# A state-space and expert layer on one core: x turned by a transfer, part of one ScalarE product given to GpSimd, and the small stages laid anew

## The reference, cut to what matters

```python
x = x[:, ::2, :]                               # 32 batches, 750 -> 375 rows, 256 wide; segments of 128
h = softmax(x @ x.T / 16) @ x                  # in each of 3 segments (the last one is padded with zeros)
# selective scan
x_in, z = split(layernorm(h) @ W_in.T)         # 512 and 512 wide
u = silu(conv4(x_in) + b_conv);  dt = softplus(u @ W_dt.T + b_dt)
Bm, Cm = u @ W_B.T, u @ W_C.T                  # 16 states each
for t in rows:                                 # for each state n of 16, each channel of 512
    hid[n] = exp(dt[t] * A[n]) * hid[n] + (dt[t] * u[t]) * Bm[t, n]
    y[t] = sum_n hid[n] * Cm[t, n]
h = h + (y * silu(z)) @ W_out.T
# experts: sigmoid scores of 64 experts, 4 of 8 groups, 8 experts per row, 256 slots each
h = h + experts(layernorm(h))
```

## Time and profile before

| | us |
|---|---|
| median of 3 runs | 3411.68 (3406.43 to 6037.72) |
| the profiled execution | 3408.89, of which 3407.0 from its first to its last instruction |
| up to the first scan | 71 |
| the 32 batches' scans | 71.3 to 2868.8 |
| rest of the sequence phase | until about 2915 |
| count and expert phases | about 2915 to 3407 |

### The profile page before, as it was taken

How to read it: one execution, slowest core, us unless ns; L and a number is a source line. 1 busy time by engine, 2 the same in 40 slices (tenths; PEclk the granted TensorE clock), 3 DMA queues, 4 the chain that set the end, 5 groups by cost and what they waited for, 6 DMA issues and landing times. The chain is left out here.

```text
span 3407.0 us, 56637 instructions
## 1 busy us (share of the span) xinstructions
PE 2969.6 (87%) x19009; PEld 2397.3 (70%) x19009; DVE 2858.1 (84%) x4628; ACT 2823.4 (83%) x5457; POOL 2105.5 (62%) x780
## 2 busy tenths in 40 slices
PE   6899999999999999999999999999999987566664
PEld 4677777777777777777777777777777776455543
DVE  4888999999999999999999999999999997444442
ACT  5999999999999999999999999999999996211110
POOL 0666666666666666666666666666666665177776
PEclk8999999999999999999999999999999998588887
DMA  2111121212112111122222212112221111377774
GB/s 94 52 52 52 55 63 63 63 63 63 58 60 63 56 52 58 63 63 63 63 63 63 64 63 63 59 59 63 63 63 63 59 54 32 94 151 147 149 149 82
DMA packets 187455, 240.52 MB, mean 71 GB/s; under 512 B 45152, under 2 KB 165440, under 8 KB 187200
## 3 DMA queue, kind: packets, MB, share of 16 engines
q1 hardware_dynamic: 162624, 199.44, 18.7%
q0 software_dynamic: 24576, 37.77, 6.6%
HBM read 176.07 MB, written 61.08 MB: 70 GB/s over the span
## 5 line engine op out<-in xcount | busy, mean ns | idle before, releaser
L360 POOL TENSOR_TENSOR hid<-hid,c_all 128x1536 f32<-128x1536 f32 x512 | 1770.4, 3458 | 1100.4 <-DVEq L616 1094.9
L621 DVE TENSOR_TENSOR_SCAN hid<-decay,hid,psB 128x1024 f32<-128x1024 f32 x512 | 1201.4, 2347 | 88.7 <-PE psB L932 42.4
L392 ACT ACTIVATE decay<-dt,a_neg 128x383 f32<-128x383 f32 x2048 | 1086.4, 606 | 0.4
L380 ACT ACTIVATE dbu_t<-dtu_t,b_t 128x512 f32<-128x512 f32 x1536 | 993.2, 714 | 7.5 <-PE psB L932 7.4
L932 PE MATMUL psB<-ident,dbu_t 128*128 128x128 f32 x6144 | 856.5, 276 | 108.4 <-DVE hid L621 102.7
L932 PEld LDWEIGHTS psB<-ident,dbu_t 128*128 128x128 f32 x6144 | 699.0, 141 | 248.5 <-issue 122.7
L944 PE MATMUL psY<-ident,hid 128*128 128x128 f32 x6144 | 757.1, 273 | 1.7 <-POOL hid L360 1.7
L944 PEld LDWEIGHTS psY<-ident,hid 128*128 128x128 f32 x6144 | 689.7, 141 | 2.0 <-POOL hid L360 1.9
L621 DVE TENSOR_TENSOR_SCAN hid<-decay,psB 128x512 f32<-128x512 f32 x512 | 623.3, 1217 | 15.5 <-PE psB L932 10.7
L1019 PE MATMUL psM<-u,w_dt 128*128 128x384 f32 x1024 | 353.2, 488 | 3.4 <-ACT u L424 2.7
L1434 ACT ACTIVATE e_side<-e_psL,e_in_tile 128x128 f32<-128x128 f32 x128 | 45.8, 363 | 260.1 <-DVE e_in_tile L1558 259.4
(11 more groups left out here) (148 smaller groups left out, 3294.3 us busy)
## 6 DMA issues: line engine op xcount, KB each, us to landing
c_all<-bc_rows_dram SPq DMA_DIRECT2D x128, 768.0 KB, 4.8
out_dram<-h SPq DMA_DIRECT2D x64, 384.0 KB, 5.6
h<-out_dram SPq DMA_DIRECT2D x32, 384.0 KB, 3.6
x_weights_dram<-normed SPq DMA_DIRECT2D x32, 384.0 KB, 2.6
xs<-in_x_dram SPq DMA_DIRECT2D x32, 256.0 KB
e_wg<-in_gate_dram SPq DMA_DIRECT2D x64, 128.0 KB, 2.7
e_wu<-in_up_dram SPq DMA_DIRECT2D x64, 128.0 KB, 3.0
e_wd<-in_down_dram SPq DMA_DIRECT2D x64, 128.0 KB, 3.4
```

The costliest lines, as they stand in the source:

```text
L360: nc.gpsimd.tensor_tensor(hid[k % 4][:, :, :], hid[k % 4][:, :, :], c_all[:, k, :].unsqueeze(1).to_broadcast([P, CH, L]), ALU.mult).then_i ...
L380: last = nc.scalar.activation(dbu_t[k % 2][:, t, :], dtu_t[q][:, t, :], ACT.Copy, scale=b_t[q][:, t, k:k + 1])
L392: last = nc.scalar.activation(decay[k % 4][:, c, 1:L], dt[q][:, c, 1:L], ACT.Exp, scale=a_neg[:, c, k:k + 1])
L621: nc.vector.tensor_tensor_scan(h[:, lo:hi], flat(decay[k % 4])[:, lo:hi], flat(psB)[:, lo:hi], h[:, lo - 1:lo] if j else 0.0, ALU.mult, AL ...
```

## The change

It does five things, all in the sequence phase.

1. **x by a transfer.** The host hands over a second, transposed copy of x (`x_t`); SP loads it into a new tile `xt` (two chunks of 128 partitions x 375). `turn_x`, QT0 and QT1 and their two copies go. The factor 1/16 moves into the scale of the softmax exponential, and `row_max` gets a second DVE instruction, on 3 columns, which multiplies by -1/16.
2. **GpSimd part.** In the states 3, 4, 12, 13 and 14 (`POOL_PART`) ACT scales two thirds of `dbu_t`, and POOL the last third, by a `tensor_tensor` with B broadcast along 512 columns. It stands on POOL's queue behind `times_c` of three states earlier. The POOL loop is unrolled.
3. **Carriers.** All `sem_inc(s_turn, 1)` go.
4. **Copies.** XN0 and XN1 are copied by ACT instead of DVE.
5. **Steps and banks.** Most small stages stand at other steps, and names at other places of the two banks.

```diff
+POOL_PART = (3, 4, 12, 13, 14,)
+SLOTTED = (("XN0", "X0", "X2T1", "X2", "Z0", "LG", "Z2", "D0", "D1", "D3", "CB", "BT", "AT1", "YT1", "X2T0",
+            "DU1", "O0"),
+           ("O1", "XN1", "X1", "X3", "Z1", "YT0", "D2", "S", "PT", "AT0", "DU0", "YT2", "DU2"))
...
+                sp.dma_start(xt[:, :, 0:(S + DIL - 1) // DIL],
+                             w["x_t"][a].rearrange("(k p) t -> p k t", p=P)).then_inc(s_x, 16)
...
+            def scaled_part(b, q, k):
+
+                s = NS * b + k
+                pool.wait_ge(s_bs, s)
+                pool.wait_ge(s_bt, PB * (s - 1))
+                t = NSEG - 1
+                nc.gpsimd.tensor_tensor(dbu_t[k % 2][:, t, :], dtu_t[q][:, t, :],
+                                        b_t[q][:, t, k:k + 1].to_broadcast([P, DI]), ALU.mult).then_inc(s_bp, 1)
 
-            with pool.Fori(0, NB) as b:
+            for b in range(NB):
                 for k in range(NS):
                     times_c(b, k)
+                    if k + 3 in POOL_PART:
+                        scaled_part(b, b % 2, k + 3)
...
-                for t in range(NSEG):
+                for t in range(NSEG - (k in POOL_PART)):
                     last = nc.scalar.activation(dbu_t[k % 2][:, t, :], dtu_t[q][:, t, :], ACT.Copy,
                                                 scale=b_t[q][:, t, k:k + 1])
...
                 if j == 0:
-                    dve.sem_inc(s_turn, 1)
-                    nc.vector.engine_nop().then_inc(s_go, 1)
+                        nc.vector.engine_nop().then_inc(s_go, 1)
...
+                nc.vector.tensor_reduce(rmax[:, :], psM[slot("S")][:, 0:L].rearrange("p (s k) -> p s k", s=NSEG),
+                                        AX.X, ALU.max).then_inc(s_rm, 1)
+                dve.wait_ge(s_rm, a + 1)
+                nc.vector.tensor_scalar(nmax[:, :], rmax[:, :], -(D ** -0.5), None, ALU.mult).then_inc(s_nm, 1)
...
                 dve.wait_ge(s_st[j], n + 1)
-                dve.sem_inc(s_turn, 1)
...
-                elif j == 0:
-                    pe.wait_ge(s_bs, SCALED * b + scaled_before(k) + 1)
+                if j == 0:
+                    pe.wait_ge(s_bs, s + 1)
+                    if k in POOL_PART:
+                        pe.wait_ge(s_bp, len(POOL_PART) * b + POOL_PART.index(k) + 1)
...
-            def turn_x(b, kd):
-                pe.wait_ge(s_x, 32 * (b + 1))
-                turn(f"QT{kd}", b, [xs[:, s, kd * P:(kd + 1) * P] for s in range(NSEG)])
-
```

More of the change, by code:

```diff
@@ L214, in number @@
             ahead = [LAG[o] - LAG[name] + (i <= at) for i, o in enumerate(names)]
-            if not isinstance(batch, int):
-                return batch * len(names) + sum(ahead)
             return sum(min(max(batch + a, 0), NB) for a in ahead)
@@ L224, in each @@
         def each(eng, body):
-            def one(b, q):
-                fixed = isinstance(b, int)
-                body(b, q, scans=not fixed or 0 <= b < NB, back=not fixed or 0 <= b - 1 < NB,
-                     late=not fixed or 0 <= b - 2 < NB, routed=not fixed or 0 <= b - 3 < NB,
-                     front=not fixed or 0 <= b + 1 < NB, early=not fixed or 0 <= b + 2 < NB)
             for b in range(-2, NB + 3):
-                one(b, b % 2)
+                body(b, b % 2, scans=0 <= b < NB, back=0 <= b - 1 < NB, late=0 <= b - 2 < NB,
+                     routed=0 <= b - 3 < NB, front=0 <= b + 1 < NB, early=0 <= b + 2 < NB)
         block = ctx.enter_context(nc.Block())
@@ L844, in body @@
                     if k == 0:
+                        if late:
+                            add_block(o, 0)
                         if front:
-                            copy_turned("XN0", n, 0)
-                            copy_turned("XN1", n, 1)
+                            newton(n, 0)
                     if k == 1:
@@ L972, in scores @@
             def scores(b):
-                for name in last_of("QT0", "QT1"):
-                    copied(name, b)
+                pe.wait_ge(s_x, 48 * (b + 1))
                 emptied("S", b)
@@ L1128, in body @@
                         if early:
-                            turn_probs(a)
+                            scores(a)
                     if k == 9:
```

253 lines of the change are left out of this document (112 added, 141 removed).

## The result

The changed kernel takes **3302.6 us** (median of 4 runs, 3298.0 to 3306.7) against 3409.1 us of the kernel before in the same session: ratio 0.969, interval 0.967 to 0.972, so 3.1% faster. (One of the four runs of the kernel before took 6037.7 us and is left out of the ratio.) Forecast were 3353 us and 1.7%. The profiled execution after takes 3304.6 us, of which 3302.7 are its span; it is 104.3 us shorter than the span before.

A forecast was written before the change was run, and what follows sets the result against it. DVE was taken to bound the scans. A full batch gains 1.42 + 1.25 - 0.80 = 1.87 us; 27 such batches give 50.5, others 5, the start 2, so 3353 us, range 3330 to 3408.

The forecast's parts named there:

- the sum of what DVE's own work loses: DVE's time per batch: copies 0.92, new product -0.20, carriers 0.60, drive's gap 0.10, in all 1.42 us.
- The phase and the bound: The scans of 32 batches hold 2797 of 3407 us; DVE bounds them, ACT and PE follow closely.
- Those ahead of a scan ... I cost them at nothing: Carriers ahead of a scan and in `choose` are passed while DVE still works; five others were costed at 0.60 us.
- All other stages of DVE only change their step; their durations stay: DVE's stages beyond copies, new product, carriers and `drive`: moving them to other steps was given no gain or loss.
- None of it is on the path: ACT's lost work, with five scalings of 3.2 us a batch: only makes ACT come less late to PE's banks.
- The GpSimd part: POOL's multiplication, tight in states 12 to 14: taken as 1.2 us each, lower bound 1.15, upper 3.46.
- The wait of 0.5 us in state 14: DVE waits 2d - 1.9 us a batch for state 14, d being POOL's part time: 0.5 us at 1.2.
- The waits in sum: DVE's new waits per batch: 0.5 in state 14, 0.1 in state 9, 0.2 unnamed; 0.8 replaces 1.25 us.
- Early batches: The first three batches lack some stages and PE leads in the first: gain of 1.0 us each.
- rival 1: The new order leaves no wait: under 0.45 us together, batch gains 2.2 to 2.67, 3327 to 3343 us; chance 0.27.
- Rival 3: POOL and DVE hold each other up at `newton`, with two SBUF operands: costs 13 us, giving 3366; chance 0.05.
- Rival 4: The part is slow on GpSimd, making states 13 and 14 wait: up to 3493 us; chance 0.07.

## Why the prediction was wrong, point by point

The step that failed is the sum of what DVE's own work loses. It was 1.42 us a batch, and 2.5 to 2.6 were measured: 0.92 for the copies, -0.20 for `row_max`, 1.0 for the carriers where 0.60 was taken, and 0.77 for the new order where 0.10 was taken.

- **The phase and the bound.** That the scans decide, and that DVE comes first with ACT and PE close behind, was right in order but too sharp. Before, DVE's queue and the way ACT, PE, `row_max` were one cycle (carriers alone: 0.78 us of own time, 0.23 of period). After, by undisturbed batches, DVE's carriers count at 0.8 of 1.0 us, and PE's work still at 0.6 of 1.0.
- **"Those ahead of a scan ... I cost them at nothing": failed.** Their waits were indeed over, but each costs 0.08 to 0.12 us behind a short instruction. All carriers are 1.0 us a batch, not 0.60.
- **"All other stages of DVE only change their step; their durations stay": failed.** The durations did stay. But what one instruction costs is from start to start, and the new order puts independent instructions between dependent ones: 0.13 (convolution), 0.23 (step 5) and 0.32 (`drive` without its hidden wait) where I had 0.10 for `drive` alone; that is 0.68 in these places, and 0.77 for the whole batch. These two steps are the missing 1.1 us of DVE's own time: 0.4 from the carriers, 0.7 from the order.
- **Copies and `row_max`.** 0.92 and -0.20: nothing measured against them; put back at step 2 the copies cost 1.0 us of DVE's own time and 0.9 of waits.
- **"None of it is on the path" (ACT's saving): failed as a statement of the changed kernel**, without changing the sum. Taken away, the part costs 1.94 us a batch, 2.5 by undisturbed ones. The forecast compared with a kernel before in which nothing needed it.
- **The GpSimd part.** 1.05 us where 1.2 was taken and 1.15 was "a lower bound". The bound was wrong by its reasoning: a proportion from the row of a larger instruction is no bound if the form differs. The wait of 0.5 us in state 14 didn't come: by the prediction's own formula 2 x 1.05 - 1.9 leaves 0.2, and back-to-back instructions on POOL start 0.04 to 0.06 us before the one ahead ends. The estimate of 1.24 from the figure of the Trainium skill (GPSIMD Engine Reference, section Elementwise, side-by-side cycle accounting) is further off; the trace has 1.05.
- **The waits in sum.** 0.86 against 0.8, by luck: an undisturbed batch has 0.3, all in state 9, and the rest came from the falls of the clock, which no term of the prediction had. The 1.25 us before mix 7.7/8 with a wait of nine batches divided by eight; an undisturbed batch before has 1.31 (0.30, 0.30 and 0.71), so this is without effect.
- **Early batches.** 4.2 us each over four periods, where I had 1.0 each for the first three batches. The first of these periods, 55.9 us in the changed kernel, is 55.7 to 58.6 in its variants with periods of 85 to 87 us, so up to 2.7 of the 16.7 us may be chance. In 265 us of this stretch DVE's waits for PE fell from 22.8 us in 28 to 12.7 in 17, so PE's relief may count more there; it wasn't taken apart further.
- **Rivals.** The time came out below rival 1's 3327. Its condition (new waits under 0.45 us) did hold in undisturbed batches, with 0.3, but alone it gives 1.42 + 1.31 - 0.3 = 2.4 us a batch of the 3.5 that these gained. Rival 3 didn't happen in this kernel but is real: 24% in its extreme, 1.3 us a batch in the kernel before with the part. It had been given 0.05; that the new order keeps POOL away from such instructions in more places than `newton` the prediction hadn't seen. Rival 4 fell: the part is fast.

Of the 46.8 us between the forecast span gain (57.5) and the real one (104.3), 28 are in the 27 steady periods (about 30 more from DVE's own time, 14 more from fewer waits, 17 less by the falls of the clock), some 14 in the first four, 5 behind the last silu.

## What to carry to other kernels

Count an in-order engine from start to start, not by durations and idle columns: a dependent pair costs 0.03 to 0.10 us of gap and 0.08 of lost overlap, a wait-only instruction up to 0.12 even when its wait is over. Look at the periods one by one before a mean is read: here a mean of 85.07 was 84.5 and falls of the clock, and a mean loss of 0.21 us hid one of 0.6. Before work is put on GpSimd, lay out beside which DVE instructions its products will end; those with two SBUF operands, and `tensor_scalar`, must not stand there, and a stage that reads one operand, moved in between, keeps them apart. When three engines are above 95%, an edit's price on one kernel isn't its price on the other: the same carriers were worth 0.2 us of an undisturbed batch before and 0.8 after.
